# Issuing the next chunk's prologue ahead of the second-half evictions, and the last two elementwise passes on GpSimd

## The reference

```python
s = attn_ref(xn)            # a second layer norm, an 8-wide linear recurrence over the sequence,
                            # W_out, a skip, a residual, a third layer norm, a 32-wide relu FFN
g = silu(ffn_ref(xn, kernel, bias))
x = x + s * g
# ffn_ref: rows of xn and columns of the 2048x2048 kernel are rounded to 8 bits,
# y = relu(xq @ kq + bq), and each row of y is rounded to 8 bits by its own maximum
```

## Time and profile before

| | us |
|---|---|
| median of 2 runs | 3808.12 (3768.32 and 3847.92) |
| profiled execution | 3775.3 |
| its span, slowest core (core 5) | 3773.8 |
| fastest core of it (core 2) | 3742.6 |
| mean granted TensorE clock, die 0 and die 1 | 0.656 and 0.648 |

### The profile page before, as it was taken

One profiled execution on the slowest core, in us unless ns is written; L12 is line 12 of the kernel. 1 busy time (PEld: TensorE's weight loads), 2 busy tenths in 40 slices (PEclk: granted clock), 3 DMA queues, 4 the chain that ended last, 5 costly groups with the idle time before them and its releaser, 6 DMA issues.

```text
span 3773.8 us, 35189 instructions; the slowest of 8 cores (3742.6 to 3773.8 us)
## 1 busy us (share of the span) xinstructions
PE 1650.2 (44%) x6049; PEld 656.7 (17%) x6049; DVE 1282.5 (34%) x3685; ACT 726.5 (19%) x869; POOL 0.2 (0%) x4
## 2 busy tenths in 40 slices
PE   2333355444444554443444444444444444344444
PEld 1222211111111111111111111111111111111111
DVE  4333333332333333333333333333333333333333
ACT  1111121222121121222212211122122221221112
POOL 0000000000000000000000000000000000000000
PEclk9999985555555556555666666666555566666666
DMA  1111100000000000000000000000000000000000
GB/s 32 45 45 44 34 9 14 23 23 23 23 23 23 23 6 17 23 23 23 23 23 23 23 23 23 23 22 2 23 23 23 23 23 23 23 23 23 23 23 12
DMA packets 56529, 87.00 MB, mean 23 GB/s; under 512 B 11118, under 2 KB 44014, under 8 KB 52206
## 3 DMA queue, kind: packets, MB, share of 16 engines
q1 hardware_dynamic: 56348, 84.75, 7.2%
HBM read 51.17 MB, written 33.55 MB: 22 GB/s over the span
## 4 chain that ended last, share of the span: by engine, by line
PE 39%; DVE 26%; issue 14%; ACT 13%; DMA 5%; DVEq 2%; SPq 1%; ACTq 0%
PE py L749 15%; DMA x<-L_attn_x 5%; PE pb L529 3%; PE pb L567 3%; PE pb L592 3%; PE pb L602 3%; PE pb L513 3%; DVE x L660 2%; DVE x2tmp L659 2%; ACT xnT L517 2%; PE pb L411 2%; PE pb L377 2%; DVE st L492 2%; ACT qi L815 2%; DVEq L73 2%
## 5 line engine op out<-in xcount | busy, mean ns | idle before, releaser
L513 PE MATMUL pb<-eyeb,xnb 128*128 128x128 bf16 x512 | 124.6, 265 | 1210.8 <-ACT xnb L491 1059.1
L749 PE MATMUL py<-kq,ixqT 128*128 128x512 bf16 x2048 | 557.0, 430 | 66.0 <-DVE t L762 65.9
L749 PEld LDWEIGHTS py<-kq,ixqT 128*128 128x128 bf16 x2048 | 216.8, 107 | 420.7 <-issue 267.1
L815 ACT ACTIVATE qi<-t,st 128x1024 int32<-128x1024 f32 x64 | 73.0, 1140 | 1088.1 <-DVE st L811 1053.7
L513 PEld LDWEIGHTS pb<-eyeb,xnb 128*128 128x128 bf16 x512 | 53.4, 104 | 1292.4 <-issue 1249.2
L759 DVE TENSOR_SCALAR_CACHE_REDUCE t<-py,st 128x512 f32<-128x512 f32 x64 | 48.0, 750 | 548.6 <-PE py L755 548.6
L677 ACT ACTIVATE sqscr<-x 128x512 f32<-128x512 f32 x128 | 80.6, 630 | 622.0 <-DVE x L660 622.0
L486 ACT ACTIVATE xn<-x,st 128x2048 f32<-128x2048 f32 x32 | 67.0, 2093 | 600.1 <-DVE st L477 600.1
L529 PE MATMUL pb<-eyeb,qbf 128*128 128x128 bf16 x512 | 125.2, 265 | 109.5 <-ACT ixqT L533 80.9
L451 DVE BATCH_NORM_STATS2 t<-x 128x6 f32<-128x512 f32 x128 | 79.1, 680 | 218.9 <-DMA x<-L_attn_x 218.9
L548 DVE CAST r1aug<-pff 1x128 bf16<-1x128 f32 x32 | 8.9, 279 | 420.8 <-PE pff L547 420.8
(11 more groups left out here) (193 smaller groups left out, 2078.6 us busy)
## 6 DMA issues: line engine op xcount, KB each, us to landing
x<-L_attn_x SPq DMA_DIRECT2D x32, 1024.0 KB, 6.0
out<-o SPq DMA_DIRECT2D x64, 512.0 KB, 3.3
xn<-L_ffn_kernel SPq DMA_DIRECT2D x128, 64.0 KB, 2.1
s<-L_ffn_kernel SPq DMA_DIRECT2D x128, 64.0 KB, 2.2
wint<-L_attn_W_in SPq DMA_DIRECT2D x16, 4.0 KB
wdnt<-L_attn_W_down SPq DMA_DIRECT2D x16, 16.0 KB
x<-L_attn_W_up SPq DMA_DIRECT2D x1, 256.0 KB
eyef<-c_eye_f SPq DMA_DIRECT2D x1, 64.0 KB
```

The source lines that it names most:

```text
L513: tlast = T(deps, lambda e, j=j, b=b: e.matmul(pb2[:, 128 * b:128 * (b + 1)], xnb_t[:, 128 * j:128 * (j + 1)], eyeb[:], start=True, stop=T ...
L749: mmlast = T(deps, lambda e, j=j, qq=qq, fofs=fofs, ixb=ixb: e.matmul(py[qq][:], ixb[:, 128 * j:128 * (j + 1)], kq[:, D * j + fofs:D * j + ...
L815: e2 = S([g5, e1[2 * h + 1], dep_q_free], lambda e, h=h: e.activation(qi_t[:], t1_t[:, 1024 * h:1024 * (h + 1)], AF.Identity, bias=0.0, sc ...
```

## The change

- `emit_schunk` is cut in three: `emit_pro(c)` (load, statistics, normalization, quantization: up to qbf), `emit_mid(c)` (transposes to s) and `emit_big_half(c, hf_)`. The evictions of a half become `emit_big_evacs(c, hf_)`. Those of the first half are still emitted directly after its matmuls.
- The loop emits, for each chunk: middle, first half and its evictions, matmuls of the second half, **the prologue of chunk c+1**, the evictions of the second half, and the output stage of chunk c. The prologue of the first chunk stands ahead of the loop.
- L829 and L833, the multiply and the add of the output stage, go from VectorE (V) to GpSimd (G): four instructions of 128x1024 fp32 per chunk.

No operation is added or removed, and no tile is added.

```diff
-        def emit_schunk(c):
+        def emit_pro(c):
...
             rc["qbf"] = V([rc["q8"], dep_qbf], lambda e: e.tensor_scalar(qbf_t[:], u8_t[:], -128.0, None, OP.add))
+            return
+
+        def emit_mid(c):
+            rc = R[c]
...
+            nwd = rc["st0"]
             dep_pT = R[c - 1].get("t2e3") if c >= 1 else KQ_READY
...
             rc["s1"] = slast
+            rc["t2e"] = t2e
+            rc["ixb"] = ixb
+            return
+
+        def emit_big_half(c, hf_):
...
+            for j in range(ND):
                 for qq in range(2):
                     fofs = 1024 * hf_ + 512 * qq
...
+            rc[f"big{hf_}"] = mmlast
+            if hf_ == 0:
+                emit_big_evacs(c, 0)
+
+        def emit_big_evacs(c, hf_):
+            rc = R[c]
+            st = st_t[c % 2]
+            dep_t1free = R[c - 1].get("e2b") if c >= 1 else None
+            e1 = rc["e1list"]
+            mmlast = rc[f"big{hf_}"]
+            e1.append(V([mmlast, rc["sc0"], dep_t1free], lambda e, hf_=hf_: e.tensor_scalar(
+                t1_t[:, 1024 * hf_:1024 * hf_ + 512], py[0][:], st[:, 12:13], None, OP.mult, OP.max,
+                accum_out=st[:, 26 + 2 * hf_:27 + 2 * hf_])))
...
-                sg = V([e4, rc["s1"], rc.get("tap_s")], lambda e, h=h: e.tensor_tensor(
+                sg = G([e4, rc["s1"], rc.get("tap_s")], lambda e, h=h: e.tensor_tensor(
                     sb_[:, 1024 * h:1024 * (h + 1)], g_t[:], sb_[:, 1024 * h:1024 * (h + 1)], OP.mult))
...
-                oo = V([sg, rc["xld"], dep_o_free], lambda e, h=h: e.tensor_tensor(
+                oo = G([sg, rc["xld"], dep_o_free], lambda e, h=h: e.tensor_tensor(
...
-        for c in (range(NCH) if TRUNC != 1 else []):
-            if c >= 1:
-                emit_echunk(c - 1)
-            emit_schunk(c)
+        if TRUNC == 0:
+            emit_pro(0)
+            for c in range(NCH):
+                emit_mid(c)
+                emit_big_half(c, 0)
+                emit_big_half(c, 1)
+                if c + 1 < NCH:
+                    emit_pro(c + 1)
+                emit_big_evacs(c, 1)
...
+                emit_echunk(c)
```

More of the change, by code:

```diff
@@ L502, in emit_schunk @@
             rc["qbf"] = V([rc["q8"], dep_qbf], lambda e: e.tensor_scalar(qbf_t[:], u8_t[:], -128.0, None, OP.add))
+            return
+        def emit_mid(c):
+            rc = R[c]
+            st = st_t[c % 2]
+            nw = nw_t[c % 2]
+            nwi = nwi_t[c % 2]
+            xn = xn_t[c % 2]
+            nwd = rc["st0"]
             dep_pT = R[c - 1].get("t2e3") if c >= 1 else KQ_READY
@@ L732, in emit_schunk @@
             rc["s1"] = slast
-            if TRUNC == 2:
-                return
+            rc["t2e"] = t2e
[3 more added lines that the diff above has]
+            rc = R[c]
+            st = st_t[c % 2]
+            t2e = rc["t2e"]
+            ixb = rc["ixb"]
             dep_y0 = R[c - 1].get("e1b") if c >= 1 else KQ_READY
             dep_t1free = R[c - 1].get("e2b") if c >= 1 else None
[L737 to L752, removed]
@@ L753, in emit_schunk @@
+            e1 = rc.setdefault("e1list", [])
+            mmlast = None
+            for j in range(ND):
                 for qq in range(2):
                     fofs = 1024 * hf_ + 512 * qq
[L755 to L764, removed]
@@ L765, in emit_schunk @@
-            rc["bigb"] = rc["big1"]
-            rc["e1b"] = e1[-1]
-            rc["e1list"] = e1
+                    deps = [t2e[j // 4], KQ_READY]
+                    if j == 0 and qq == 0:
+                        deps.append(dep_y0 if hf_ == 0 else e1[-1])
+                        deps += [rc["x2a3"], rc["x2b3"]]
+                        if c == 0:
+                            deps += [p_c8, p_cw2, p_cSe, p_wow]
+                    mmlast = T(deps, lambda e, j=j, qq=qq, fofs=fofs, ixb=ixb: e.matmul(
+                        py[qq][:], ixb[:, 128 * j:128 * (j + 1)],
+                        kq[:, D * j + fofs:D * j + fofs + 512],
+                        start=(j == 0), stop=False, skip_group_check=True), inc=False)
@@ new lines, in emit_big_half @@
+            for qq in range(2):
+                fofs = 1024 * hf_ + 512 * qq
+                mmlast = T([mmlast, rc["auge"], p_bq2], lambda e, qq=qq, fofs=fofs: e.matmul(
+                    py[qq][:], augrow[c % 2][:], bqrow[:, fofs:fofs + 512],
+                    start=False, stop=True, skip_group_check=True), inc=(qq == 1))
+            rc[f"big{hf_}"] = mmlast
+            if hf_ == 0:
+                emit_big_evacs(c, 0)
+        def emit_big_evacs(c, hf_):
+            rc = R[c]
+            st = st_t[c % 2]
+            dep_t1free = R[c - 1].get("e2b") if c >= 1 else None
[4 more added lines that the diff above has]
+                accum_out=st[:, 26 + 2 * hf_:27 + 2 * hf_])))
+            e1.append(V([e1[-1]], lambda e, hf_=hf_: e.tensor_scalar(
+                t1_t[:, 1024 * hf_ + 512:1024 * (hf_ + 1)], py[1][:], st[:, 12:13], None, OP.mult, OP.max,
+                accum_out=st[:, 27 + 2 * hf_:28 + 2 * hf_])))
+            if hf_ == 1:
+                rc["bigb"] = rc["big1"]
+                rc["e1b"] = e1[-1]
@@ L847, in build_nc @@
             R[NCH - 1]["store"] = R[NCH - 1]["store1"]
-        for c in (range(NCH) if TRUNC != 1 else []):
-            if c >= 1:
-                emit_echunk(c - 1)
-            emit_schunk(c)
[L852 to L855, removed]
+        if TRUNC == 0:
[7 more added lines that the diff above has]
+                emit_big_evacs(c, 1)
+                if DEBUG_TAPS and c == 0:
+                    dsdbg = nc.dram_tensor("dbg_s", [128, D], F32, kind="ExternalOutput").ap()
+                    R[0]["tap_s"] = dma("d_t", [R[0]["s1"]], dsdbg[:], s_t[0][:])
+                emit_echunk(c)
+        elif TRUNC != 1:
+            for c in range(NCH):
+                if c >= 1:
+                    emit_echunk(c - 1)
+                emit_pro(c)
+                if TRUNC != 21:
+                    emit_mid(c)
+                if TRUNC == 3:
+                    emit_big_half(c, 0)
+                    emit_big_half(c, 1)
+                    emit_big_evacs(c, 1)
             emit_echunk(NCH - 1)
```

## The result

The changed kernel takes 3222.15 us (median of 11 runs). The kernel before, in 10 runs, has a median of 3796.82 us. The ratio is 0.8515, 95% interval 0.848 to 0.855: 14.8% faster. That ratio leaves out slow runs on either side; in five of the 11 runs the cores of one die had a lower mean granted clock (0.647 to 0.667 for 0.684) and the die ended 24 to 46 us after the other. The prediction was 3234 us, in a range of 3212 to 3318.

What follows compares the result with a forecast made beforehand. No engine near full; a chain of waits, serial at the turn between chunks, bounds the kernel. Savings of 22 x 16.7 and 9 x 19.7, together 545 us, off 3775.3, plus 4 at the end, gave 3234 us, range 3212 to 3318.

Steps and rivals of the forecast that it cites:

- The load: Next chunk's load, put ahead of the stores, is early by some 50 us; the 7.22 us wait in each turn goes.
- Prologue and late eviction: Second-half evictions stand on VectorE behind the next prologue: 19.5 us after the first, 9.2 us late and on the path.
- GpSimd's pass: Each output-stage pass on GpSimd was taken as 2.29 us, making the second L824 start at 6.21 us, 0.28 late.
- What the move buys: Output-stage passes taken off VectorE no longer keep the next prologue waiting: 2.9 us, at no cost on the path.
- The turn: First-half eviction to the next chunk's first copy (L517): 30.0 us for 46.7.
- The end: After the last chunk the output stage is bare, with four GpSimd passes in one queue: +3.6 us.
- The clock: TensorE's granted clock starts each chunk as cold as before, at 0.50; no gain counted.
- GpSimd at 4.6 us or more: Rivals on output-stage passes: 4.58 us each, about 3315 us, chance 0.10; or so slow that GpSimd decides, chance 0.05.
- The late load: Rival: the load is not early, its 7.2 us stay in each turn, 3458 us; chance 0.02.
- More chunks at 0.81: Rival: all 22 later chunks get the 0.81 clock, product's first half about 1.0 us longer, +22, 3256 us; chance 0.13.

Runs made afterwards that it cites:

- e3: Kernel before, with only the load of the next chunk issued ahead of the output stage and stores of the chunk before; 3533.91 us, 0.936 of the kernel before.
- e5: Changed kernel, with the next chunk's transposes and their copies emitted ahead of the output stage; 2873.53 us, 0.763 of the kernel before.
- e1: Changed kernel, with the four elementwise passes back on VectorE, so the new order alone; 3214.96 us, 0.8535 of the kernel before.
- e6: e5 with the four elementwise passes on VectorE instead of GpSimd; 3137.51 us.
- e11: Changed kernel, with two one-column ScalarE instructions added between the second L824 and the next chunk's first copy; 3248.94 us.

## Why the prediction was right

**The load.** As predicted. It is issued 50 us before use: the one issued at 2458.18 is for the chunk whose L451 starts at 2508.19. Alone it is worth 6.8 us a turn (e3), 7.2 predicted.

**Prologue and late eviction.** 19.32 us between the evictions on average, 19.5 predicted; the eviction to L839 takes 3.10, as before. That the delay lies on the path only through ScalarE's queue is shown by e5, where the same late eviction costs nothing.

**GpSimd's pass.** 2.34 us, 2.29 taken. The second L848 starts 6.57 us after L839, 6.21 predicted. The Trainium skill's figure (GPSIMD Engine Reference, section 3, Performance versus the Vector engine) halves to an estimate of 2.25 us; the trace is 0.09 us above it and the ratio to VectorE is 1.9. Its advice against such passes on GpSimd holds for the changed kernel (e1, 7 us) and not for the one where VectorE has work behind them (e6).

**What the move buys.** This step was wrong in its reason. It gave the move to GpSimd 2.9 us a turn, for no longer keeping the next prologue waiting. In the new order the passes stand behind that prologue on whichever engine; e1 has them on VectorE and the same period. The 2.9 us belong to the order. The sum of the turn was right all the same, because it was made by walking the new queues and not by adding up parts.

**The turn.** 29.80 us, 30.0 predicted.

**The end.** From L839 at 3202.58 to the end of the last add at 3216.57:

```profile
3202.58 1.15 ACT L839 ACTIVATE qi<-t,st 128x1024 int32<-128x1024 f32 x1 [32.69 <-DVE st L835]
...
3214.23 2.34 POOL L857 TENSOR_TENSOR o<-s,x 128x1024 f32<-128x1024 f32 x1 [0.27 <-POOL s L853]
```

That is 13.99 us against the 9.94 of the earlier trace rows: +4.1, +3.6 predicted.

**The clock.** "The same cold start of each chunk, and no gain" was a little off. The first half fell from 11.85 to 11.46 us in the held periods, 22 x 0.39 = 9 us. The experiments say that this is not a gain of the change as such: in kernels with other turns the first half is 11.8 to 12.4 us. The changed kernel happens to be held near the low edge of what the first half can be (11.2 us is the least seen), and e11 shows that 0.53 us more in the turn loses it. So these 9 us were luck; the prediction has no term for them. In all, the 31 periods take 3133.75 - 482.78 = 2651 us, where the prediction's (22 x 85.7 + 9 x 86.6) make 2665; that is the 12 us between 3234 and 3222, to within 2 us.

**The rivals.** GpSimd at 4.6 us or more: out, by its rows. The late load: out. More chunks at 0.81: not in the changed kernel's profiled execution. Some of its windows of 4 us have a mean of 0.81, but these hold the rise from 0.50 to 1.00, as narrower ones show:

```profile
1048.00:1052.00 4.00, 4.00 (x17) 1.62 (x16) 0.65 (x1) 0.00 (x0) 0.00 (x0) 0.81 0.02 4
1049.00:1050.00 1.00, 1.00 (x5) 0.35 (x4) 0.00 (x0) 0.00 (x0) 0.00 (x0) 0.73 0.00 0
1050.00:1051.00 1.00, 1.00 (x6) 0.49 (x5) 0.00 (x0) 0.00 (x0) 0.00 (x0) 1.00 0.00 0
```

But e1 shows it and its price. Die 0 had a clock of 0.655 there and ended 28 us later than die 1; the prediction had worked out 22. Windows of its core 0, over the end of a second half:

```profile
2008.00:2012.00 4.00, 4.00 (x15) 1.55 (x14) 2.25 (x14) 0.00 (x0) 0.00 (x0) 0.72 0.01 2
2012.00:2016.00 4.00, 2.70 (x10) 0.76 (x8) 1.78 (x1) 3.84 (x2) 0.00 (x0) 0.81 0.00 0
```

Cores 0 and 1 are at 0.81 in chunks 10 to 31 and cores 2 and 3 in chunks 0 to 23; each is at 1.00 in its other chunks. The turn is 29.3 to 29.4 us at either clock, so the slower second half is hidden, as predicted. The first half is 13.1 us at 0.81 for 11.9, 1.2 us a chunk where the prediction had 1.0, and 22 to 24 such chunks are 26 to 29 us.

All four cores of the die had the lower mean clock and ended within 1 us of each other, and the other die had none of it. That agrees with the rule that was cited in the prediction (the Trainium skill, TensorE: Matmul & The Clock Gate, Part 1, a limit that takes a die to 13/16). The prediction held against that rule, since core 6 is at 1.00 where cores 4 and 5 are at 0.81. That was a misreading: the times of each core count from the start of its own span, and nothing in the traces says that these starts are one moment. In the same execution cores 6 and 7 have their stretch at 0.81 too, in chunks 18 to 26. Core 7 of the kernel before:

```profile
2390.00:2394.00 4.00, 4.00 (x17) 1.66 (x16) 0.00 (x0) 0.00 (x0) 0.00 (x0) 0.81 0.00 0
```

From its first to its last row at 0.81 that stretch is 852 us long on core 7 (2386 to 3238) and 870 us on core 5 (536 to 1407). That it is one and the same stretch, met by cores that started at different moments, is likely and not shown. What sets the 0.81 off in one execution and not in another no run here shows.

## What to carry to other kernels

Where each engine's queue keeps its order, walk the new order from event to event and take its length; do not add up what the parts seem to save. The early prologue delayed an eviction by 9 us and was right all the same, since it removed more than that from the path, and the delay itself could be made free by changing what stood behind it in a third queue. Moving a pass to a slower engine pays by what it unblocks: the same move cost 7 us in one order, 4.7% in another (3 to 4% on the cores whose loads did not land later) and gained 264 us in a third.

## What the runs showed of the hardware beyond that

The period of the loop does not follow each change of its path. With turns of 29.80, 29.35 and 28.88 us it is 85.35, 85.32 and 85.34 us, and with 39.64 and 39.07 it is 95.59 and 95.58, all with a spread of 0.34 us or less: the moment at which the granted clock rises from 0.50 in the product's first half moves the other way against the chunk, and that half takes up the difference, between about 11.2 and 12.9 us. Just outside such a range the time jumps by more than the change (+0.53 us in the turn: +27 us in all, for 16) or falls by less, and the first halves of neighbouring chunks differ by up to 1.6 us. So a small edit here can measure as nothing or as more than one and a half times its size, and an experiment that adds a delay to price a wait should be read by the stretches of its trace, not by its total alone. That it is the clock and not another resource is shown by the first halves, 8.92 us and half of the time to the rise in all kernels, and by the 85.33 us from rise to rise in the held ones. Why the rises keep that distance was not isolated.
